# Local attention: the norms of q and k moved behind the scores of the next slot, ScalarE's and VectorE's orders to match

## What is computed

```python
for i in range(6):                                  # DEPTH
    x = attn_layer(shift_tokens(x), Wqkv[i], q_scale[i], k_scale[i], Wo[i]) + x
    x = ffn_layer(shift_tokens(x), ln_g[i], ln_b[i], W1[i], b1[i], W2[i], b2[i]) + x

def attn_layer(x, Wqkv, qs, ksc, Wo):               # 16 heads of 64
    q, k, v = split_heads(x @ Wqkv)
    q = l2norm(q) * qs;  k = l2norm(k) * ksc
    q = q * cos * scale + rotate_half(q) * sin * scale
    k = k * cos / scale + rotate_half(k) * sin / scale
    return local_attention(q, k, v) @ Wo            # windows of 32 keys and the 32 before

def ffn_layer(x, g, bln, W1, b1, W2, b2):
    a, gate = split((layernorm(x) * g + bln) @ W1 + b1)
    return a * gelu(gate) @ W2 + b2
```

## Time and profile before

| | us |
|---|---|
| timed, median of 2 (2797.91 to 2800.23) | 2799.07 |
| the profiled execution | 2788.98 |
| its span in the profile | 2787.2 |
| TensorE busy in the span | 2354.2 (84%) |
| VectorE busy | 1980.3 (71%) |
| ScalarE busy | 1898.5 (68%) |
| GpSimd busy | 1081.4 (39%) |
| mean granted TensorE clock | 0.945 |

### The profile page before, as it was taken

How to read it: one execution, slowest core, us unless ns; L and a number is a source line. 1 busy time by engine, 2 the same in 40 slices (tenths; PEclk the granted TensorE clock), 3 DMA queues, 4 the chain that set the end, 5 groups by cost and what they waited for, 6 DMA issues and landing times. The chain is left out here.

```text
span 2787.2 us, 65659 instructions
## 1 busy us (share of the span) xinstructions
PE 2354.2 (84%) x25708; PEld 1190.9 (43%) x25708; DVE 1980.3 (71%) x2597; ACT 1898.5 (68%) x2977; POOL 1081.4 (39%) x461
## 2 busy tenths in 40 slices
PE   7788889888988888888898898888888878777778
PEld 2344444444444444444444444444444432222355
DVE  5577777777777776777777776777777738999642
ACT  4677777777777777777777777777777746545633
POOL 0344444444443444444443444444443402556220
PEclk8799999999999999999999999999999988999989
DMA  0100000000000000000000000000000010000001
GB/s 20 51 2 2 2 13 21 9 2 2 13 13 15 4 2 13 13 9 10 2 13 13 9 10 2 2 24 10 10 2 1 2 35 0 0 0 0 17 16 46
DMA packets 16019, 29.89 MB, mean 11 GB/s; under 512 B 3616, under 2 KB 6064, under 8 KB 15664
## 3 DMA queue, kind: packets, MB, share of 16 engines
q1 hardware_dynamic: 15760, 25.78, 3.0%
HBM read 24.73 MB, written 1.05 MB: 9 GB/s over the span
## 5 line engine op out<-in xcount | busy, mean ns | idle before, releaser
L750 POOL TENSOR_TENSOR f_shuf<-f_shuf,f_tabs 128x1024 f32<-128x1024 f32 x192 | 452.6, 2357 | 1293.0 <-DVE f_shuf L788 1293.0
L754 POOL TENSOR_TENSOR f_rot<-f_rot,f_shuf 128x1024 f32<-128x1024 f32 x192 | 452.2, 2355 | 27.5
L475 PE MATMUL f_ps<-f_sq,f_same 64*64 64x512 f32 x768 | 218.6, 641 | 264.6 <-ACT f_o L679 255.6
L700 ACT ACTIVATE f_ps<-f_s 128x512 f32<-128x512 f32 x192 | 115.6, 602 | 279.6 <-DVE f_s L815 279.4
L520 PEld LDWEIGHTS f_ps<-f_ptz,f_v 64*64 64x64 f32 x6144 | 259.1, 133 | 93.5 <-issue 93.5
L652 ACT ACTIVATE f_cross<-f_ps 64x512 f32<-64x512 f32 x384 | 226.9, 591 | 91.7 <-PE f_ps L464 86.4
L520 PE MATMUL f_ps<-f_ptz,f_v 64*64 64x96 f32 (+1 forms) x6144 | 285.4, 243 | 1.9 <-ACT f_ptz L672 1.6
L802 DVE SCALAR_TENSOR_TENSOR f_qk<-f_rn,f_rot 128x1024 f32<-128x1024 f32 x192 | 233.9, 1218 | 70.4 <-POOL f_rot L754 70.0
L788 DVE STREAM_SHUFFLE f_shuf<-f_ps 128x1024 f32<-128x1024 f32 x192 | 249.9, 1302 | 0.9
L811 DVE TENSOR_REDUCE f_max<-f_ps 128x8 f32<-128x512 f32 x192 | 131.9, 687 | 154.8 <-PE f_ps L498 153.3
L463 PE MATMUL f_ps<-f_xs,f_wq 128*128 128x512 f32 x384 | 228.6, 679 | 14.5 <-DVE f_xs L769 8.6
(11 more groups left out here) (267 smaller groups left out, 4051.5 us busy)
## 6 DMA issues: line engine op xcount, KB each, us to landing
e_w<-in_e_w SPq DMA_DIRECT2D x16, 256.0 KB, 2.8
f_wq<-in_f_wq SPq DMA_DIRECT2D x12, 256.0 KB, 2.7
f_wk<-in_f_wk SPq DMA_DIRECT2D x12, 256.0 KB, 3.4
f_wv<-in_f_wv SPq DMA_DIRECT2D x12, 256.0 KB, 4.5
f_wo<-in_f_wo SPq DMA_DIRECT2D x6, 512.0 KB, 4.1
f_w<-in_f_w SPq DMA_DIRECT2D x6, 341.0 KB, 2.9
s_dx<-in_k_pick SPq DMA_DIRECT2D x1, 1536.0 KB, 9.0
f_w<-in_f_w SPq DMA_DIRECT2D x6, 192.0 KB, 3.4
```

The lines of the kernel that those rows point to most:

```text
L475: mm = pe.matmul(view(ps, NBANK[h] * CH, [1, CH], p0=64 * (h if own else 1 - h), rows=64), same_head[k, k], of, start=True, stop=True, ski ...
L750: pool.tensor_tensor(view(shuf, 0, [S, 4], [1, S]), view(shuf, 0, [S, 4], [1, S]), view(tab_s, 0, [S, 2], [0, 2], [1, S]), ALU.mult).then_ ...
L754: pool.tensor_tensor(rot[:, :], rot[:, :], shuf[:, :], ALU.add).then_inc(sem["rot"], 1)
```

## The change

`norms` of pair j+2 leave the end of TensorE's slot j. They now stand in the following slot, where the pair is j+1, behind the scores (and behind `wo_part(6, 8)` in slot 2 and gates 1 and 2 in slot 6) and before the projection. `inverse_norm` is cut in two: `norm_log` stands before the softmax exponential on ScalarE, `norm_exp` between it and the squares. VectorE does `soft_b` before `normalise` and not behind it. Gate 0 goes to bank 2 (the turn's) and not to 6: it waits for `spread(4)`, and `turn(5)` waits for its gelu; the waits for bank 6 go.

```diff
--- before.py
+++ after.py
@@ -337,7 +337,7 @@
         bank = lambda k, n=1: view(ps, k * CH, *([[CH, n]] if n > 1 else []), [1, CH])
 
         Y0, H0_, G0 = NU, 1, 1
-        GBANK = (6, 0, 1)
+        GBANK = (2, 0, 1)
         NBANK = (6, 7)
 
 
@@ -441,8 +441,6 @@
                 need(pe, sem[f"wv{q // 4}"], (i // NU) * 16 + 16)
                 need(pe, sem["v"], i * 8 + q)
                 need(pe, sem["ln"], i * 8 + q)
-                if q == 0:
-                    need(pe, sem["gelu"], i * 3 - 6 + 1 + G0)
                 for r in range(2):
                     for h in range(2):
                         at = 128 * (q % 4) + 64 * r
@@ -503,6 +501,8 @@
             def turn(i, j):
                 need(pe, sem["p"], i * 8 + j + 1)
                 need(pe, sem["ptz"], i * 8 + j)
+                if j == 5:
+                    need(pe, sem["gelu"], i * 3 - 3 + 1 + G0)
                 for t in range(4):
                     mm = pe.transpose(view(ps, 2 * CH + 128 * t, [1, 128]), s[j % 2][:, 128 * t:128 * t + 128], ident[:, :])
                 mm.then_inc(sem["t_mm"], 1)
@@ -570,6 +570,7 @@
                 k = i - 1
                 has, u, a = (run, i, j + 2) if j < 6 else (more, i + 1, j - 6)
                 had1, u1, b1 = (run, i, j - 1) if j >= 1 else (before, k, 7)
+                next1, u3, a3 = (run, i, j + 1) if j < 7 else (more, i + 1, 0)
                 had2, u2, b2 = (run, i, j - 2) if j >= 2 else (before, k, j + 6)
                 if run:
                     scores(i, j)
@@ -581,6 +582,8 @@
                     need(pe, sem["straight"], i * 8 + 8 if run else 0)
                     gate_mm(k, 1)
                     gate_mm(k, 2)
+                if next1:
+                    norms(u3, a3)
                 if j == 6 and had2:
                     mix(u2, b2)
                 if has:
@@ -601,14 +604,11 @@
                     hid_mm(k, 2)
                 if had1:
                     turn(u1, b1)
-                if has:
-                    norms(u, a)
                 if before and j == 4:
                     variance(k)
                 if before and j == 5:
                     hid_mm(k, 0)
-                    if run:
-                        need(pe, sem["ln"], i * 8 + 8)
+                    need(pe, sem["ptz"], i * 8 + 5 if run else i * 8)
                     gate_mm(k, 0)
                 if before and j == 7:
                     w2_mm(k)
@@ -652,12 +652,15 @@
                         ins = act.activation(to, view(ps, (h if own else 1 - h) * CH, [1, CH], p0=64 * h, rows=64), ACT.Square)
                 ins.then_inc(sem["sq"], 1)
 
-            def inverse_norm(i, j):
+            def norm_log(i, j):
 
                 need(act, sem["n_mm"], i * 8 + j + 1)
                 need(act, sem["qk"], i * 8 + j)
                 act.activation(view(rn, 0, [UNIT, 2], [1, UNIT]), bank(NBANK[0], 2), ACT.Ln,
                                scale=float(2.0 ** 20)).then_inc(sem["ln"], 1)
+
+            def norm_exp(i, j):
+
                 need(act, sem["ln"], i * 8 + j + 1)
                 act.activation(rn[:, :], rn[:, :], ACT.Exp, scale=-0.5, bias=con.lift).then_inc(sem["rn"], 1)
 
@@ -695,10 +699,14 @@
                     gelu(k, 1)
                     gelu(k, 2)
                     nc.scalar.preload_act_table_set(ACT_SET)
+                if next1:
+                    norm_log(u3, a3)
                 if run:
                     need(act, sem["shift"], i * 8 + j + 1)
                     act.activation(view(ps, 4 * CH, [CH, 2], [64, 4], [1, 64]), view(s[j % 2], 0, [64, 2], [128, 4], [1, 64]),
                                    ACT.Exp, scale=8.0).then_inc(sem["exp"], 1)
+                if next1:
+                    norm_exp(u3, a3)
                 if has:
                     square(u, a)
                 if before and j == 4:
@@ -713,8 +721,6 @@
                     out_copy(u2, b2)
                 if had1:
                     spread(u1, b1)
-                if has:
-                    inverse_norm(u, a)
                 if before and j == 4:
                     need(act, sem["var"], k + 1)
                     act.activation(sq2[:, :], bank(3), ACT.Ln, bias=con.eps).then_inc(sem["ln2"], 1)
@@ -847,14 +853,14 @@
                     hidden(k, 0)
                 if before and j == 7:
                     hidden(k, 2)
+                if run:
+                    soft_b(i, j)
                 if next1:
                     normalise(u1, a1)
                 if j == 6 and more:
                     tables(i + 1)
                 if before and j == 6:
                     hidden(k, 1)
-                if run:
-                    soft_b(i, j)
                 if has:
                     shuffle(u, a)
                     straight(u, a)
```

## The result

| | before | after |
|---|---|---|
| timed, median of 2 (us) | 2799.07 (2797.91 to 2800.23) | 3021.01 (3017.29 to 3024.74) |
| span of the profiled execution | 2787.2 | 3023.0 |
| mean granted TensorE clock | 0.945 | 0.907 |
| mean of 21 units of the steady loop, w2 to w2 | 89.9 | 101.1 |

The changed kernel is slower: ratio 1.079 (95% interval 1.073 to 1.085), +222 us against the +51 forecast. 21 units of 11.2 us more make 235 us, which is the difference of the spans (235.8); the first unit and the ends nearly cancel.

A forecast was written before the change was run, and what follows sets the result against it. TensorE bounds slots 0 and 1; in slots 2 to 5 it waits for a ScalarE and VectorE chain. Terms of +4.0 us and 0.9 low clock make 92.6 against 90.1 per unit: +57, first unit -6, so 2850 us, range 2785 to 2930.

The forecast's parts named there:

- first unit: The unit without FFN work: a slot takes 8.1 us instead of 9.00, -6 us over the unit.
- scores(2) to soft_a(3): Slot 2 into 3: softmax exponential queued behind the norms' Ln, then rn exponential and squares; 14.21 to 16.19 us, +1.98.
- soft_a(3) to soft_a(4): Slot 3 into 4: the squares stand behind one more instruction, the rn exponential; before 8.97 us, +1.07.
- xn to scores(6): Slot 5 into 6: exponential and spread now stand ahead of gate(0); 9.86 us before without low clock, +0.2.
- scores(6) to scores(7): Slot 6: mix(4), ahead of the projection, waits for the Ln of norms(7); 11.26 to 12.25 us, +0.99.
- scores(7) to scores(0): Slot 7 to the loop's turn: values wait for the Ln of norms(0); before 12.62 us with 0.77 issue, +1.13.
- slots 0 and 1: Start of the unit, bound by TensorE's own work: 19.7 us, unchanged, 0.
- third term: soft_a(4) to xn: ScalarE no longer waits for norms before the variance's Ln; 10.99 to 9.62 us, -1.37.
- low clock: TensorE at 1.2 GHz behind idle gaps: 0.9 us per unit after the change, bounds 0 and 2.4.
- No change: Rival for the whole kernel: the order only moves the wait, idle sum equal; 2799 us, chance 0.08.
- faster by TensorE: Rival: the norms' wait goes and nothing replaces it, TensorE bounds; 2554 us, chance 0.12.
- xn loses to GpSimd: Rival: xn waits 2.4 us more behind GpSimd's second operation, and low clock stays; 2925 us, chance 0.22.

The follow-up runs named there:

- 19 waits: Changed kernel with 19 instructions of already granted waits on TensorE ahead of its loop, putting the head at 2275 as before the change: 2909.7 us, ratio 1.0415.
- after_warm: Changed kernel with 19 waits, plus two unused filling products ahead of the variance and two ahead of hid(0): 2875.7 us, ratio 1.0303.
- experiment 2: Changed kernel with 19 waits, TensorE's order in slots 6 and 7 made projection, values, mix: 2837.8 us; the same order in the kernel before: 2843.1 us.
- both moves: Changed kernel with 19 waits, projection ahead of mix (slot 6) and values (slot 7), and wo_part(6, 8) behind the projection in slot 2: 2780.8 us, ratio 0.9947.
- experiment 3: Changed kernel with 19 waits, wo_part(6, 8) moved behind the projection in slot 2: 2878.2 us; with both moves 2780.8 us.
- 128 waits: Changed kernel with 128 instructions of satisfied waits ahead of TensorE's loop, its head at 2384: 3030.0 us, ratio 1.084.
- combo_warm: Kernel with both moves, plus four unused filling products ahead of the variance and hid(0): 2773.2 us, ratio 0.9926.

## Why the prediction was wrong

**The sign was right, and so was the mechanism of slots 2 to 5.** The wait that goes is worth nothing, as the recurrence there gets longer. The terms, measured in the unit above (scores(2) at 1310.31, soft_a(3) 1326.45, soft_a(4) 1336.50, xn 1346.05, scores(6) 1356.01), and as means of the changed kernel and of the same with 19 waits:

| stretch | forecast | this unit | changed | with 19 waits |
|---|---|---|---|---|
| scores(2) to soft_a(3) | 16.19 | 16.14 | 16.16 | 16.15 |
| soft_a(3) to soft_a(4) | 10.04 | 10.05 | 10.04 | 10.04 |
| soft_a(4) to xn | 9.62 | 9.55 | 9.56 | 9.54 |
| xn to scores(6) | 10.06 | 9.96 | 10.61 | 10.83 |
| scores(6) to scores(7) | 12.25 | 13.93 | 14.29 | 14.36 |
| scores(7) to scores(0) | 13.75 with 0.77 issue | 17.78 | 17.44 | 14.39 |
| slots 0 and 1 | 19.7 | 22.42 | 22.77 | 20.19 |

The third term was forecast as a gain. It came because xn won against GpSimd by 0.09 us, which was luck as much as reckoning, as the forecast called it a dead heat:

```profile
1346.05 0.69 DVE L881 TENSOR_TENSOR f_xn<-f_cen,f_sq 128x512 f32<-128x512 f32 x1 [1.39 <-ACT f_sq L728]
```

```profile
1346.14 2.82 POOL L760 TENSOR_TENSOR f_rot<-f_rot,f_shuf 128x1024 f32<-128x1024 f32 x1
```

**The step that failed** is the term "scores(7) to scores(0)", into which the 0.77 us of issue was carried over unchanged, together with slots 0 and 1, "TensorE's own work, 19.7 us, unchanged". The issue gap measured 4.4 us on average (4.1 to 5.3), and slots 0 and 1 took 22.8 us at the low clock behind it. I took the gap at the loop's turn as a constant of the loop. It depends on where the head falls in the instruction packets, and a change of the work ahead of the loop moves that. No rival had it. It is worth 114 us, and it alone put the time out of the range: 2907 us lies in it. Without it the change still costs 110 to 117 us beside the kernel before on the same chip, over twice the +51.

**The low clock** was the second miss: 0.9 us a unit taken, out of bounds of 0 to 2.4. With the place mended the unit is 95.5, and 91.7 was its structure, so 3.8 us remain. By the last column 0.8 of them are xn to scores(6), 2.1 scores(6) to scores(7), 0.6 scores(7) to scores(0) and 0.5 slots 0 and 1. In after_warm the first two take 9.95 and 12.78 us, so 2.5 of their 2.9 are clock. In the unit of slot 6 shown in experiment 2, mix(4) takes 2.12 us instead of 1.49, and the projection of q behind it 2.07 instead of 1.12, behind the wait of 2.33 us, at the place where the work behind it is on the path. In slot 7 0.5 is the issue gap (1.28 us on average where 0.77 was taken), in slots 0 and 1 it is gaps of 0.2 to 0.3 us ahead of the norms, which now directly follow the scores. The upper of my two bounds was thus the better guide; I had chosen by the length of the gaps and not by what stands behind them.

**"No change" and "faster by TensorE"** were rightly set low. **xn loses to GpSimd** was the right mechanism with the wrong place: in the changed kernel 1 of 24 loses, but once the chain is shortened it decides over units: in the kernel with both moves (experiment 3) those with a long xn take 92.0 us from scores(0) to scores(0), the others 89.1.

**The first unit** was forecast 6 us shorter. The first w2 comes at 266.5 us against 270.1 (262.2 with 19 waits), so 4 and 8.

Still open: what makes the first packet of a turn start 0.9 us later behind w2 in the new order than in the old, with the head at the same number; and which gaps bring the low clock in one unit and not in the next.

## What to carry to other kernels

Read the gap at a loop's turn as a quantity that any edit ahead of the loop or of the loop's head can change, and when a change moves the time by more than its own terms do, count the instruction packets (one more per turn was the sign of a head just short of a packet's end; the kernel with 128 waits, bad in another way, has 242 too) and shift the loop by a few granted waits before looking for a reason in the order. A new wait is to be priced with the clock that follows it and by what stands behind it: a gap ahead of work with slack costs nothing (the variance), the one ahead of mix(4), with the low clock behind it, 1.6 to 2.1 us a unit. Two remedies that do nothing or little alone can be worth 1% together, so try them together where traces show both losses.

## What the runs showed of the hardware

- **Instruction packets.** At a loop's turn TensorE fetches a packet of 16 KB, and the next one starts about 3.3 us later (3.0 to 4.5). If the head is at most 4 instructions short of a packet's end (2256 is bad, 2260 good), the products wait for both: gaps of 2.7 to 5.3 us instead of 0.1 to 2.2, one packet more per turn (263 for 242), and 5.2 to 5.6 us a turn with the low clock behind the gap, in either kernel. The Trainium skill, page "Runtime: NRT & Kernel Launch", section "Instruction fetch mechanics", says that instructions are refilled in blocks of 256 and that a taken branch outside the window forces a fetch. The trace agrees on both: each turn starts with a packet, and heads at 2256 and 2512 behave alike. It adds what the place of the target costs.
- **VectorE's product of two SBUF tensors beside GpSimd's.** The one that starts first runs on; a start of 0.11 us behind costs xn 2.1 us (in combo_warm one of 0.02 us too), one of 0.08 us ahead costs GpSimd 0.47. The Trainium skill, page "SBUF — State Buffer", section "Who interferes with whom", has it that the order of issue decides who blocks: the trace agrees, and xn ended 0.55 us behind GpSimd's end in place of the 0.69 it takes alone.
- **The clock.** The variance product took 1.12 us in one unit and 2.07 in another, at 2.4 and at 1.2 GHz, behind nearly equal idle time (2.29 and 2.34 us).
